# A three-round graph kernel: the rest rows of split chunks fetched by SyncE, where it fetched whole chunks

## The chip, the cores and the metric

The kernel runs on one core of a Trainium2 chip. The metric is the device time of one execution in microseconds (us); lower is better. Engines are called as in the profile: PE (TensorE), DVE (VectorE), ACT (ScalarE), POOL (GpSimd) and SP (SyncE).

## The reference

A graph has 12,500 nodes with 128 features and 200,000 edges, sorted by target node, each edge with a source node, one of four types and a weight. Cut to what matters:

```python
h = relu(layernorm(x))
ew = (w - w.min()) / (w.max() - w.min() + 1e-8)
# convolution 1 and 2 (relu between them): each edge takes its source's row,
# multiplied by the matrix of the edge's type, weighted, summed at the target
m = sum_r (type == r) * (h[src] @ W[r]);  out = segment_sum(m * ew, dst) + h @ root + b
x = x + conv2(relu(conv1(h)))
h = relu(layernorm(x))
x = x + segment_sum(w * h[src], dst) @ W3.T + b3
```

So there are three rounds over all edges, r = 0, 1, 2, and each must gather one row of 512 bytes for each edge.

## The kernel before

**Tiling.** The 200,000 edges are cut into 1,563 chunks of 128 edges (P = 128). Four chunks are a group (CG = 4), four groups a unit (UG = 4, UC = 16 chunks), and there are 98 units in a round (NU = 98). A ring of four units (RING = 4) of gathered rows stands in SBUF as `rows`, with 64 slots of 128 partitions by 128 floats.

**Gathering.** For each chunk POOL issues one indirect DMA (`gather`, L558), which reads 128 row numbers from a column of `idx` and brings 128 rows of 512 bytes from a table in HBM to one slot of `rows`. The tables are `table0` (round 0; its first four units gather from x), `table1` (round 1) and `table2` (round 2). DVE writes `idx` when a slot's unit of the last turn of the ring is done, and POOL waits for it (`s_idx`). At the second chunk of each group POOL also waits until PE has begun the group two before it (`paced`, `s_begun`, LEAD = 2).

**What POOL does not gather.** In units with u % 4 == 3 (`by_sp`; not u = 3 of round 0) the whole chunk 12 (SK) is fetched by SP: 128 DMAs of one row each, with addresses loaded from a list into registers eight at a time (`single_rows`, L502). They go to one of two buffers `spare`, and SP spreads them over the four units before (`singles`, a quarter of the 128 in each). In rounds 1 and 2, ACT fetches chunk 12 of units 17, 25, ... in the same way (`act_rows`, `spare_a`). That makes 71 chunks of SP, 22 of ACT, and 3 x 1,563 - 93 = 4,596 gathers of POOL.

**Use.** PE waits for each chunk's rows (`wait_rows`) and multiplies them with a window matrix that DVE built (L975 in round 0, L1016 in rounds 1 and 2). DVE adds the group's sums to `acc`. Tiles of nodes are then finished by PE, ACT and DVE, and SP stores them to the next table or to the output (`table1_out`, `table2_out`, `out_pair`). A round's gathers can begin only when the table before is complete.

**Order on SP.** SP's program has one order. In the setup: loads of x and of the edge lists, the weights, two lists for SP's own chunks and two for ACT's (`s_single_list`), then the 15 stores of `table0` (L418), each after ACT's `s_tab`. DVE waits for all four lists (`s_single_list` at 64) before it turns them to byte addresses (L1194 and following), and then starts on round 0. In the rounds, each unit's stores and loads are followed by the unit's share of single rows (`singles(r, u)`).

Of the kernel before, what the change touches and what calls it, by code (L numbers as in the profile page):

```python
# [4 lines left out]
P = 128  # L5
CG = 4
# [7 lines left out]
EARLY = 6  # L14
OB = 8
SE = 4
AE = 8
LEAD = 2
SETTLED = 12
# [4 lines left out]
def build(nc, x, src, dst, etype, weight, W1, root1, b1, W2, root2, b2, W3, b3, out):  # L24
# [44 lines left out]
    with ctx:  # L69
# [3 lines left out]
        def sem(name):  # L73
            return ctx.enter_context(nc.semaphore(name))
# [86 lines left out]
        s_single = [[sem(f"s_single{r}{b}") for b in range(2)] for r in range(3)]  # L161
        s_single_at = sem("s_single_at")
        s_single_list = sem("s_single_list")
        s_by_act = [sem(f"s_by_act{b}") for b in range(2)]
        s_idx_part, s_agg_part = sem("s_idx_part"), sem("s_agg_part")

# [66 lines left out]
        def by_sp(r, u):  # L233

            return u % SE == SE - 1 and (r > 0 or u >= SE)

        def is_single(r, u, k=SK):

            return k == SK and (by_sp(r, u) or by_act(r, u))

        def by_act(r, u):

# [19 lines left out]
        def wait_rows(eng, r, u, k):  # L262

            if u == NU - 1:
                eng.wait_ge(s_tail[k], 16 * (r + 1))
            elif is_single(r, u, k) and by_act(r, u):
                n = act_number(r, u)
                eng.wait_ge(s_by_act[n % 2], 16 * P * (n // 2 + 1))
            elif is_single(r, u, k):
                n = single_number(r, u // SE)  # L270
                so_far = len(range(n, single_number(r, 0 if r else 1) - 1, -2))
                eng.wait_ge(s_single[r][n % 2], 16 * P * so_far)
            elif k == SK:
                eng.wait_ge(rows_signal(u, k), single_gathers(r, u))
            elif k % CG < CG - 1:
                v = u % RING
                per_round = NI if v < last_units - 1 else NI - 1
                both = 2 if k % CG == CG - 2 else 1
                eng.wait_ge(s_row[v * UG + k // CG][k % CG], 16 * both * (r * per_round + u // RING + 1))

        def chunk_rows(r, u, k):

            if is_single(r, u, k) and by_act(r, u):
                return spare_a[:, act_number(r, u) % 2, :]
            if is_single(r, u, k):
                return single_buffer(single_number(r, u // SE))
            return rows[:, u % RING * UC + k, :]

        def paced(r, u, k):
# [63 lines left out]
        def _(eng):  # L353
# [127 lines left out]
            def single_rows(r, j, lo, hi):  # L481

                n = single_number(r, j)
                if lo == 0:
                    if n == 0:
                        eng.wait_ge(s_single_at, 7)
                    elif n > 1:
                        r0, j0 = divmod(n - 1, NO)
                        u = j0 * SE + SE - 1
                        if r0 == 0:  # L490
                            eng.wait_ge(s_half, 2 * u + 2)
                        else:
                            eng.wait_ge(s_agg, (r0 - 1) * NU + u + 1)
                numbers, table = single_at[r], in_bytes[r]
                to = single_buffer(n).bitcast(mybir.dt.uint8)
                for p in range(lo, hi, OB):
                    found = nc.values_load_multi_w_load_instructions(
                        numbers[j:j + 1, p:p + OB], engines=(mybir.EngineType.SP,), min_val=0,
                        max_val=table.shape[1] - row_bytes,
                        skip_runtime_bounds_check_because="the lists name nodes of the graph alone")[1]  # L500
                    for k in range(OB):
                        eng.dma_start(to[p + k:p + k + 1, :], table[0:1, bass.ds(found[k], row_bytes)]  # L502
                                      ).then_inc(s_single[r][n % 2], 16)

            def singles(r, u):

                if u < 2:
                    if r > 0:
                        single_rows(r, 0, u * P // 2, (u + 1) * P // 2)
                else:  # L510
# [36 lines left out]
        def _(eng):  # L547
# [9 lines left out]
            def gather(table, slot, signal):  # L557
# [291 lines left out]
        def _(eng):  # L849
# [99 lines left out]
            def first_round():  # L949
# [6 lines left out]
                def unit(i, v):  # L956
                    u = i * RING + v
                    for q in range(UG):
                        h = q // 2
                        if q in groups_of(u):  # L960
# [3 lines left out]
                            for k in range(n):  # L964
                                if not raw:
                                    wait_rows(eng, 0, u, q * CG + k)
                                if k == 0 and (raw or g == RING * UG):
# [31 lines left out]
            def fast(r):  # L999

                def unit(i, v):
# [5 lines left out]
                    for q in groups_of(u):  # L1007
# [3 lines left out]
                        for k in range(n):  # L1011
                            slot = v * UC + q * CG + k
                            wait_rows(eng, r, u, q * CG + k)
                            if k == CG - 1 and q == UG - 1 and RING - 1 <= u < NU - 1:
                                eng.wait_ge(s_window, u * 2 + ((r - 1) * 2 * NU + 4))
                            ins = eng.matmul(agg_of(u, v, q)[:, q * W:(q + 1) * W], chunk_rows(r, u, q * CG + k), window[:, slot, :],  # L1016
# [53 lines left out]
        def _(eng):  # L1070
# [446 lines left out]
```

## Time and profile before

| what | value |
|---|---|
| time, median of 2 runs | 7904.76 us (7901.24 to 7908.29) |
| profiled execution, first to last instruction (span) | 5774.9 us |
| POOL busy in the span | 4343.6 us, 75% |
| PE busy | 3158.5 us, 55% |
| DVE, ACT busy | 25%, 8% |
| gathers of POOL | 4,596 |
| one-row DMAs of SP, of ACT | 9,088 and 2,816 |

The span is 2,130 us shorter than the median of the runs. The profile shows nothing of what lies around the span, and no separate time of that one execution; the span is all that is known of it. Busy time of POOL counts its gathers while descriptors are made; "issue" is idle time in which an engine waited for nothing that the profile shows.

### The profile page before, as it was taken

What the parts mean: (1) busy time and instruction counts of PE and PEld (TensorE: products, weight loads), DVE (VectorE), ACT (ScalarE), POOL (GpSimd) and SP (SyncE); (2) the same over time, 40 slices, a digit from 0 to 9 for tenths busy, and PEclk for the clock granted to TensorE, in tenths of its full rate; (3) what the DMA queues carried; (4) which work ended last, traced back from release to release, by engine and by line L of the source; (5) the groups of instructions that cost most, each with busy time, mean ns of one, the idle gap of its engine ahead of it and who ended that gap; (6) DMA issues with size and microseconds to landing.
All of it is one profiled execution on the core that took longest, in us unless ns stands there. A gap on an engine that the chain in (4) does not pass through costs nothing.

```text
span 5774.9 us, 61089 instructions
## 1 busy us (share of the span) xinstructions
PE 3158.5 (55%) x11399; PEld 2521.8 (44%) x11399; DVE 1415.7 (25%) x5042; ACT 439.1 (8%) x1183; POOL 4343.6 (75%) x4604
## 2 busy tenths in 40 slices
PE   3766666666666545444444444444444445444454
PEld 2655544544555434333334443434444444444443
DVE  7433333333333222122212222211111111111111
ACT  5111111111111000000000000000000000000000
POOL 7777777777777677777777777777777777777777
PEclk7878788788877655555555555555555555555555
DMA  6222222222222222222222222222222222222222
GB/s 173 82 76 74 73 75 74 73 75 74 73 75 74 61 62 62 61 60 62 62 60 61 62 62 60 62 59 60 62 62 60 62 62 60 62 62 61 60 62 58
DMA packets 285830, 392.59 MB, mean 68 GB/s; under 512 B 92011, under 2 KB 199360, under 8 KB 285440
## 3 DMA queue, kind: packets, MB, share of 16 engines
q0 software_dynamic: 147072, 301.50, 20.0%
q1 hardware_dynamic: 132736, 85.70, 4.9%
q14 instruction: 299, 2.45, 0.1%
q8 instruction: 91, 1.49, 0.1%
q10 hardware_dynamic: 5632, 1.45, 0.1%
HBM read 336.95 MB, written 51.34 MB: 67 GB/s over the span
## 4 chain that ended last, share of the span: by engine, by line
POOL 74%; issue 24%; PE 1%; DMA 1%; DVE 0%; ACT 0%; POOLq 0%; DVEq 0%
POOL rows L558 74%; DMA rows<-table,idx 1%; PE bank L975 0%; PE bank L915 0%; PE bank L893 0%; PE bank L908 0%; PE bank L923 0%; DMA table<-st 0%; DMA table<-sums 0%; DMA st<-in_src_dram 0%; PE bank L924 0%; DVE win L1342 0%; PE bank L1016 0%; DVE acc L1223 0%; POOLq L69 0%
## 5 line engine op out<-in xcount | busy, mean ns | idle before, releaser
L558 POOL DMA_INDIRECT rows<-table,idx x4532 | 4276.9, 944 | 1402.1 <-issue 1378.0
L1016 PE MATMUL bank<-win,rows 128*128 128x48 f32 x6112 | 1816.9, 424 | 1938.7 <-DMA rows<-table,idx 1917.4
L1016 PEld LDWEIGHTS bank<-win,rows 128*128 128x128 f32 x6112 | 1474.6, 317 | 2281.5 <-DMA rows<-table,idx 2261.1
L975 PE MATMUL bank<-win,rows 128*128 128x192 f32 x3080 | 850.0, 404 | 634.9 <-DMA rows<-table,idx 490.2
L975 PEld LDWEIGHTS bank<-win,rows 128*128 128x128 f32 x3080 | 587.4, 226 | 846.9 <-DMA rows<-table,idx 670.2
L1223 DVE TENSOR_TENSOR acc<-acc,bank 128x48 f32 x1173 | 237.8, 203 | 1106.0 <-PE bank L893 956.6
L1342 DVE TENSOR_SCALAR win<-iota,key,sw_col 128x192 f32<-128x192 f32 x1563 | 501.5, 391 | 18.2 <-PE bank L908 16.2
L688 ACT ACTIVATE tile_T<-acc 128x128 f32<-128x128 f32 x196 | 60.4, 309 | 2852.5 <-DVE acc L1223 2852.5
L1285 DVE TENSOR_SCALAR idx<-src_col 128x16 int32<-128x16 int32 x98 | 18.5, 191 | 829.7 <-PE bank L1016 829.7
L893 PE MATMUL bank<-sums,W1s 128*128 128x192 f32 (+1 forms) x784 | 218.7, 445 | 0.4 <-ACT sums L736 0.4
L1372 DVE TENSOR_TENSOR bank<-bank,rel 128x384 f32<-128x384 f32 x392 | 218.6, 558 | 0.7 <-issue 0.2
L1292 DVE SCALAR_TENSOR_TENSOR idx<-src_col,type_col 128x16 int32<-128x16 int32 x98 | 18.5, 191 | 772.1 <-PE bank L1016 772.1
L893 PEld LDWEIGHTS bank<-sums,W1s 128*128 128x128 f32 x784 | 205.1, 280 | 0.9 <-ACT sums L736 0.9
L1273 DVE TENSOR_TENSOR st<-bank,x_rows 128x128 f32<-128x128 f32 x98 | 28.6, 292 | 709.3 <-PE bank L947 709.3
L1094 DVE BATCH_NORM_STATS2 stats<-bank 128x6 f32<-128x128 f32 x98 | 29.2, 299 | 677.9 <-PE bank L945 677.9
L915 PE MATMUL bank<-W2s,tile_T 128*128 128x512 f32 x194 | 147.9, 858 | 0.0
L1376 DVE TENSOR_TENSOR win<-bank,w_col 128x384 f32<-128x384 f32 x196 | 109.0, 556 | 6.8
L1376 DVE TENSOR_TENSOR win<-bank,sw_col 128x384 f32<-128x384 f32 x196 | 109.0, 556 | 6.8
L623 ACT ACTIVATE std<-mv,eps 128x1 f32<-128x1 f32 (+3 forms) x127 | 37.2, 293 | 822.3 <-DVE mv L1100 822.3
L701 ACT ACTIVATE acc<-bank,b2s 128x128 f32<-128x128 f32 x98 | 36.0, 367 | 740.8 <-PE bank L924 740.8
L736 ACT ACTIVATE sums<-bank 128x384 f32<-128x384 f32 x196 | 85.6, 495 | 5.6 <-PE bank L975 5.6
L678 ACT ACTIVATE hT<-bank 128x128 f32<-128x128 f32 x98 | 27.2, 277 | 756.6 <-PE bank L901 756.6
(123 smaller groups left out, 1235.4 us busy)
## 6 DMA issues: line engine op xcount, KB each, us to landing
spare<-table SPq DMA_DIRECT2D x9088, 0.5 KB
rows<-table,idx POOLq DMA_INDIRECT x4532, 2.5
spare_a<-table ACTq DMA_DIRECT2D x2816, 0.5 KB
table<-st SPq DMA_DIRECT2D x146, 256.0 KB, 2.4
x_rows<-table SPq DMA_DIRECT2D x49, 128.0 KB
x_rows<-in_x_dram SPq DMA_DIRECT2D x48, 128.0 KB
h_rows<-table SPq DMA_DIRECT2D x48, 128.0 KB, 2.3
out_dram<-st SPq DMA_DIRECT2D x48, 128.0 KB, 2.1
```

The lines of the kernel that those rows point to most:

```text
L558: eng.indirect_dma_start(out=rows[:, slot, :], out_offset=None, in_=table[:, :], in_offset=bass.IndirectOffsetOnAxis(ap=idx[:, slot:slot + ...
L623: eng.activation(std[:, p, 0:n], mv[:, p, 0:n, 1], ACT.Sqrt, bias=eps[:, 0:1]).then_inc(s_std, 1)
L688: eng.activation(tile_T[:, s, :], columns(t), ACT.Copy).then_inc(s_prep, 1)
L736: eng.activation(sums[:, v % 2, 2 * h:2 * h + w, :].rearrange("p g w -> p (g w)"), half_ps[v % 2 * 2 + h][:, 0:w * RW], ACT.Copy).then_inc ...
L893: ins = eng.matmul(mix_ps[:, 0:w], W1s[:, k, :], rhs(k), start=(k == 0), stop=(k == R - 1))
L915: eng.matmul(wide_of(t)[:, :], inner_of(t, s), W2s[:, :, :].rearrange("p r d -> p (r d)"), start=True, stop=True).then_inc(s_fin, 1)
L975: ins = eng.matmul(half_ps[v % 2 * 2 + h][:, q % 2 * RW:(q % 2 + 1) * RW], chunk_rows(0, u, q * CG + k), wide[:, v % 2, q * CG + k, :], st ...
L1016: ins = eng.matmul(agg_of(u, v, q)[:, q * W:(q + 1) * W], chunk_rows(r, u, q * CG + k), window[:, slot, :], start=(k == 0), stop=(k == n - 1))
L1223: eng.tensor_tensor(a, a, sums_ps, ALU.add).then_inc(s_acc, 1)
L1342: ins = eng.tensor_scalar(wide[:, v % 2, q * CG + k, :], iota[:, 0:RW], key0[:, bass.ds(c, 1)], sw_col[:, bass.ds(c, 1)], ALU.is_equal, AL ...
L1372: eng.tensor_tensor(match_ps[:, 0:n, :], iota_ps.unsqueeze(1).to_broadcast([P, n, W]), rel[:, bass.ds(c + lo, n)].unsqueeze(2).to_broadcas ...
L1376: eng.tensor_tensor(slots, match_ps[:, 0:n, :], wt[:, bass.ds(c + lo, n)].unsqueeze(2).to_broadcast([P, n, W]), ALU.mult).then_inc(s_windo ...
```

## The change

In each unit with u % 4 == 3 (again not u = 3 of round 0) POOL now issues a gather for all 16 chunks. In m of the 16 chunks the gather covers only the first n rows, and SP fetches the other 128 - n rows of these chunks, one DMA for each row, straight into their places in `rows`. The pair (m, n) goes through (1, 64), (2, 96), (4, 112), (8, 120), (16, 124), (16, 126), (16, 127) from one such unit to the next, so SP fetches 64, 64, 64, 64, 64, 32 and 16 rows of a unit, not 128. The chunks are 0, 16/m, 2 x 16/m and so on.

SP fetches a unit's rows in its program order at the two units u - 4 and u - 3, and only once PE is done with the unit that used the same slots (u - 4). PE waits for them at the unit's chunk 0 (`wait_parts`); before, it waited at chunk 12. In the setup the two lists are loaded by 2 + 48 small DMAs, with a wait of SP for the first two (`s_single_first`), and DVE waits for all of them. ACT's chunks stay as they are.

```diff
+PARTS = ((1, 64), (2, 96), (4, 112), (8, 120), (16, 124), (16, 126), (16, 127))
...
-            return k == SK and (by_sp(r, u) or by_act(r, u))
+            return k == SK and by_act(r, u)
+        def parts(u):
+            m, n = PARTS[u // SE % len(PARTS)]
+            return range(0, UC, UC // m), n
+        def rows_by_pool(r, u, k):
+            if not by_sp(r, u):
+                return P
+            of, n = parts(u)
+            return n if k in of else P
...
+        def wait_parts(eng, r, u, k):
+            if by_sp(r, u) and k == parts(u)[0][0]:
+                n = single_number(r, u // SE)
+                mine = range(n, single_number(r, 0 if r else 1) - 1, -2)
+                eng.wait_ge(s_single[r][n % 2], 16 * sum(rows_by_sp(r, ((i + 1) - r * NO) * SE + SE - 1) for i in mine))
...
-                              ).then_inc(s_single_list, 16)
+                              ).then_inc(s_single_first, 16)
+            eng.wait_ge(s_single_first, 32)
+            for to, arr in ((single_src, src), (single_type, etype)):
+                for j in range(NO):
+                    u = j * SE + SE - 1
+                    of, n = parts(u)
+                    eng.dma_start(to[j:j + 1, 0:len(of) * (P - n)].rearrange("a (m e) -> a m e", m=len(of)),
+                                  arr[u * UC * P:(u + 1) * UC * P].rearrange("(m c e) -> m c e", m=len(of), e=P)[:, 0, n:P].unsqueeze(0),
+                                  allow_slow_non_contiguous=n == P - 1).then_inc(s_single_list, 16)
...
-                for p in range(lo, hi, OB):
+                for p in range(lo, min(hi, len(of) * each), OB):
...
-                        eng.dma_start(to[p + k:p + k + 1, :], table[0:1, bass.ds(found[k], row_bytes)]
-                                      ).then_inc(s_single[r][n % 2], 16)
+                        slot, row = u % RING * UC + of[(p + k) // each], by_pool + (p + k) % each
+                        to = rows[row:row + 1, slot, :].bitcast(mybir.dt.uint8)
+                        eng.dma_start(to, table[0:1, bass.ds(found[k], row_bytes)]).then_inc(s_single[r][n % 2], 16)
...
-                if u < 2:
-                    if r > 0:
-                        single_rows(r, 0, u * P // 2, (u + 1) * P // 2)
-                else:
-                    j, part = divmod(u + 2, SE)
-                    if 0 < j < NO:
-                        single_rows(r, j, part * P // SE, (part + 1) * P // SE)
+                j, part = divmod(u + 1, SE)
+                if j < NO and by_sp(r, j * SE + SE - 1) and part < 2:
+                    single_rows(r, j, 0 if u == 0 else part * P // 4, (part + 1) * P // 4)
...
-                    out=rows[:, slot, :], out_offset=None, in_=table[:, :],
-                    in_offset=bass.IndirectOffsetOnAxis(ap=idx[:, slot:slot + 1], axis=0)).then_inc(signal, 16)
+                    out=rows[0:n, slot, :], out_offset=None, in_=table[:, :],
+                    in_offset=bass.IndirectOffsetOnAxis(ap=idx[0:n, slot:slot + 1], axis=0)).then_inc(signal, 16)
...
-                        gather(table, v * UC + k, rows_signal(u, k))
+                        gather(table, v * UC + k, rows_signal(u, k), rows_by_pool(r, u, k))
...
-            eng.wait_ge(s_single_list, 64)
+            eng.wait_ge(s_single_list, 32 + 32 * NO)
```

## Rows read from the trace of the kernel before

**Rows 1.** The page: the chain that ended last, by engine, then by line.

```profile
POOL 74%; issue 24%; PE 1%; DMA 1%; DVE 0%; ACT 0%; POOLq 0%; DVEq 0%
```

**Rows 2.** The source line L558: durations ns min/median/max, releasers (us, times), landing.

```profile
L558 POOL DMA_INDIRECT rows<-table,idx x4532: 940/944/1071, 88.1 to 5765.9; - x198
...
  issue: 1397.2, 4581
  DMA table<-sums: 12.0, 1
  DMA table<-st: 8.5, 1
  PE bank L975: 3.7, 12
...
DMA to landing us min/median/max: 2.4/2.5/7.0
```

**Rows 3.** Timeline of POOL in round 2: start us, us, instruction, idle before it.

```profile
5000.57 0.95 POOL L558 DMA_INDIRECT rows<-table,idx  x1 [0.30 <-issue]
...
5041.79 0.95 POOL L558 DMA_INDIRECT rows<-table,idx  x1 [0.30 <-issue]
```

**Rows 4.** Windows of 500 us, one in each round: busy us (count) by engine, clock, DMA.

```profile
1000.00:1500.00 500.00, 333.77 (x1245) 250.12 (x1245) 158.31 (x550) 58.92 (x154) 377.73 (x402) 0.82 0.27 74
2500.00:3000.00 500.00, 247.24 (x845) 199.29 (x846) 102.88 (x381) 27.28 (x77) 377.65 (x402) 0.50 0.23 61
4500.00:5000.00 500.00, 247.58 (x872) 205.84 (x872) 82.89 (x259) 8.04 (x26) 378.02 (x401) 0.50 0.23 61
```

**Rows 5.** Waits, all engines: who waited for whom, us, times, longest.

```profile
PE bank L1016 <- DMA rows<-table,idx: 1917.4, 1773, 7.9
```

**Rows 6.** The page: DMA queues, packets, MB, share of 16 engines' span.

```profile
q0 software_dynamic: 147072, 301.50, 20.0%
```

**Rows 7.** Timeline of SP's queue at the start of round 1 and in it.

```profile
1944.15 45.84 SPq L502 DMA_DIRECT2D spare<-table  x105
```

**Rows 8.** Waits of SP's queue, whole span: us, times, longest.

```profile
SPq L471 <- DVE st L1273: 514.8, 46, 39.0
SPq L444 <- DVE st L1238: 473.7, 46, 38.5
SPq L428 <- ACT st L712: 424.2, 85, 19.7
```

**Rows 9.** Timeline of SP's queue in the setup.

```profile
12.93 0.23 SPq L372 DMA_DIRECT2D win<-in_src_dram  x1
...
44.31 0.40 SPq L409 DMA_DIRECT2D single_src<-in_src_dram  x1
...
46.02 30.67 SPq L418 DMA_DIRECT2D table<-acc  x15
79.79 16.92 SPq L388 DMA_DIRECT2D h_rows<-table  x3
```

**Rows 10.** Waits of SP's queue from 0 to 320 us.

```profile
SPq L418 <- ACT acc L628: 20.2, 8, 2.9
```

**Rows 11.** The page: a first load's size and time to landing.

```profile
st<-in_src_dram SPq DMA_DIRECT2D x1, 64.0 KB, 1.8
```

**Rows 12.** Timeline of DVE in the setup and the first unit.

```profile
71.09 0.42 DVE L1194 TENSOR_SCALAR single_at<-single_src 24x128 int32<-24x128 int32 x1
...
84.35 0.23 DVE L1301 COPY idx<-src_col 128x8 int32<-128x8 int32 x1
```

**Rows 13.** Timeline of POOL at its first gather from table0.

```profile
86.87 0.94 POOL L558 DMA_INDIRECT rows<-in_x_dram,idx  x1 [0.30 <-issue]
88.12 0.94 POOL L558 DMA_INDIRECT rows<-table,idx  x1 [0.30 <-issue]
```

More of the change, by code:

```diff
@@ L163, in build @@
         s_single_list = sem("s_single_list")
+        s_single_first = sem("s_single_first")
         s_by_act = [sem(f"s_by_act{b}") for b in range(2)]
@@ L237, in is_single, with rows_by_sp @@
         def is_single(r, u, k=SK):
-            return k == SK and (by_sp(r, u) or by_act(r, u))
+            return k == SK and by_act(r, u)
[7 more added lines that the diff above has]
+            return n if k in of else P
+        def rows_by_sp(r, u):
+            of, n = parts(u)
+            return len(of) * (P - n)
         def by_act(r, u):
@@ L268, in wait_rows @@
                 eng.wait_ge(s_by_act[n % 2], 16 * P * (n // 2 + 1))
[L269 to L272, printed above, removed]
             elif k == SK:
@@ L284, in chunk_rows @@
                 return spare_a[:, act_number(r, u) % 2, :]
-            if is_single(r, u, k):
-                return single_buffer(single_number(r, u // SE))
             return rows[:, u % RING * UC + k, :]
@@ L409, in _ @@
                 eng.dma_start(to[:, :], arr[0:last].rearrange("(j c e) -> j c e", c=SE * UC, e=P)[:, (SE - 1) * UC + SK, :]
-                              ).then_inc(s_single_list, 16)
+                              ).then_inc(s_single_first, 16)
[3 more added lines that the diff above has]
+                    u = j * SE + SE - 1
+                    of, n = parts(u)
+                    eng.dma_start(to[j:j + 1, 0:len(of) * (P - n)].rearrange("a (m e) -> a m e", m=len(of)),
+                                  arr[u * UC * P:(u + 1) * UC * P].rearrange("(m c e) -> m c e", m=len(of), e=P)[:, 0, n:P].unsqueeze(0),
+                                  allow_slow_non_contiguous=n == P - 1).then_inc(s_single_list, 16)
             for to, arr in ((act_src, src), (act_type, etype)):
@@ L483, in single_rows @@
                 n = single_number(r, j)
+                u = j * SE + SE - 1
+                of, by_pool = parts(u)
+                each = P - by_pool
                 if lo == 0:
@@ L486, in single_rows @@
                         eng.wait_ge(s_single_at, 7)
[L487 to L491, printed above, removed]
-                        else:
-                            eng.wait_ge(s_agg, (r0 - 1) * NU + u + 1)
+                    r0, before = (r, u - RING) if u >= RING else (r - 1, u + (NU - 1) // RING * RING - RING)
+                    if r0 == 0:
+                        eng.wait_ge(s_half, 2 * before + 2)
+                    else:
+                        eng.wait_ge(s_agg, (r0 - 1) * NU + before + 1)
                 numbers, table = single_at[r], in_bytes[r]
-                to = single_buffer(n).bitcast(mybir.dt.uint8)
-                for p in range(lo, hi, OB):
+                for p in range(lo, min(hi, len(of) * each), OB):
                     found = nc.values_load_multi_w_load_instructions(
@@ L501, in single_rows @@
                     for k in range(OB):
-                        eng.dma_start(to[p + k:p + k + 1, :], table[0:1, bass.ds(found[k], row_bytes)]
-                                      ).then_inc(s_single[r][n % 2], 16)
+                        slot, row = u % RING * UC + of[(p + k) // each], by_pool + (p + k) % each
+                        to = rows[row:row + 1, slot, :].bitcast(mybir.dt.uint8)
+                        eng.dma_start(to, table[0:1, bass.ds(found[k], row_bytes)]).then_inc(s_single[r][n % 2], 16)
             def singles(r, u):
-                if u < 2:
-                    if r > 0:
-                        single_rows(r, 0, u * P // 2, (u + 1) * P // 2)
-                else:
-                    j, part = divmod(u + 2, SE)
-                    if 0 < j < NO:
-                        single_rows(r, j, part * P // SE, (part + 1) * P // SE)
+                j, part = divmod(u + 1, SE)
+                if j < NO and by_sp(r, j * SE + SE - 1) and part < 2:
+                    single_rows(r, j, 0 if u == 0 else part * P // 4, (part + 1) * P // 4)
             for u in range(NU):
@@ L555, in _, with gather @@
                      allow_small_or_imprecise_dtypes=True).then_inc(s_const, 1)
-            def gather(table, slot, signal):
+            def gather(table, slot, signal, n=P):
                 eng.indirect_dma_start(
-                    out=rows[:, slot, :], out_offset=None, in_=table[:, :],
-                    in_offset=bass.IndirectOffsetOnAxis(ap=idx[:, slot:slot + 1], axis=0)).then_inc(signal, 16)
+                    out=rows[0:n, slot, :], out_offset=None, in_=table[:, :],
+                    in_offset=bass.IndirectOffsetOnAxis(ap=idx[0:n, slot:slot + 1], axis=0)).then_inc(signal, 16)
             def gather_unit(table, r, i, v):
@@ L966, in unit @@
                                     wait_rows(eng, 0, u, q * CG + k)
+                                    wait_parts(eng, 0, u, q * CG + k)
                                 if k == 0 and (raw or g == RING * UG):
@@ L1013, in unit @@
                             wait_rows(eng, r, u, q * CG + k)
+                            wait_parts(eng, r, u, q * CG + k)
                             if k == CG - 1 and q == UG - 1 and RING - 1 <= u < NU - 1:
```

## The prediction

> **What bounds the kernel now.** I read the chain of work that ended last first: 74% of it is POOL and 24% is issue, the stretches before POOL's own gathers; nothing else reaches 2% [rows 1]. Then the gather's source line: each of the 4,532 gathers from a table takes 940 to 1,071 ns, median 944, and nearly all the idle time ahead of them is issue, 1,397 us in 4,581 pieces, so 0.305 us each [rows 2]. The timeline gives the sum directly: from 5000.57 to 5041.79 us there are 33 gathers, 41.22 / 33 = 1.249 us from one start to the next [rows 3]. The windows say that this holds in all rounds, whatever PE does: 401 or 402 gathers in every 500 us, with PE at 334 us busy in round 0 and at 247 in the others, and at a granted clock of 0.82 or 0.50 [rows 4]. 4,596 x 1.249 = 5,740 us of a span of 5,775. The rest is the start and the two table changes, where POOL waited 12.0 and 8.5 us [rows 2]. The waits show the other side: PE stood 1,917 us for gathered rows in rounds 1 and 2 alone [rows 5]. So POOL sets the span by the number of gathers and by what one costs.
>
> The timed runs are 7,905 us, 2,130 more than the span, and no view says what that is. I take it as a part that the change leaves alone, and carry the other reading as a rival. The sum below is made on the span and then added to 7,905. This kernel's measurement can tell about 2% (158 us) from no change.
>
> **The change: POOL.** Before, POOL left out one chunk in each of 71 units (24 in a round, 23 in round 0). Now it leaves out none: 71 more gathers, 4,667 in all. At 1.249 us each that is +88.7 us, all on the path, since POOL waits for nothing else.
>
> Against that stand shorter gathers. In seven such units 1 + 2 + 4 + 8 + 16 + 16 + 16 = 63 gathers are cut, by 368 rows in all. A round has three such turns and the first three units of a fourth: 196 cut gathers and 1,296 rows; over the kernel, less the one unit of round 0, 587 gathers and 3,824 rows. Every gather of the trace has 128 rows, so the price of a row is bounded only: if the length doesn't depend on rows, 0; if all of the 1.249 us does, 9.76 ns a row, 37.3 us in all; and if the 944 ns busy alone do, 7.4 ns and 28.2 us. The narrow band of 940 to 1,071 ns [rows 2] says that the cost is software of fixed length, but not in which loop. I take half of the busy part, 14 us, and keep 0 and 37. A gather of an odd number of rows might instead cost more than one of 128; no row excludes it and no row prices it, so it goes to the rivals.
>
> The first thing to see here is that leaving out one whole chunk takes 1.249 us off POOL for 128 rows of SP, while the same SP rows spread over many gathers take at most that and perhaps nothing. The Trainium skill ("DMA: Bandwidth & Descriptors", section "Anatomy of one DMA — SWDGE (gpsimd) path") calls descriptor generation small and variable and says that one can emit a lot of descriptors before the incremental cost shows up. By that rule the saving is 0 and the POOL term 88.7 in place of 74.6; the trace has one size of gather only and neither agrees nor disagrees.
>
> **SP and the new wait.** SP's one-row DMAs fall from 9,088 to 3,824. One costs SP 45.84 / 105 = 0.437 us with its address loads [rows 7]. That frees 5,264 x 0.437 = 2,300 us of SP, none of it on the path: SP already waited over 1,400 us for tiles to store [rows 8]. Gain 0.
>
> Of a unit u, SP now starts only when PE has finished u - 4, since the rows go into ring slots. It then needs at most 64 x 0.437 = 28 us plus a landing of about 2.5 us. PE wants them at chunk 0 of unit u, three units or 47 gathers later, 47 x 1.249 = 59 us (48 if ACT fetches none). Cover: 28 us to spare; without it PE would wait and POOL would follow after its lead. Behind the waiting SP stand the stores of finished tiles and the reloads of `x_rows`; those of rounds 1 and 2 come up to one unit (20 us) later. They have two staging slots of a pair of tiles each, 40 us of work a turn, and SP's waits of up to 39 us for tiles [rows 8] show it far ahead. Price 0; at worst, some us at the end of a round, but the last unit with SP rows is 95 and its rows are issued at 91 and 92. So the table changes stay at 12.0 and 8.5 us.
>
> PE's own work is the same matmuls, and its waits are filled by POOL's pace; 0.
>
> **The setup.** SP gets a wait and 48 list DMAs ahead of the stores of table0. The nearest issue times are 0.23 us for a one-row load and 0.40 for the 24-row list [rows 9]: 11 to 19 us. The wait costs about a landing, 1.8 us [rows 11], plus little. The stores started at 46.0 and would start at 59 to 68. They took 30.7 us [rows 9], of which 20.2 were waits for ACT [rows 10], so 10.5 us of issue alone: at worst they end at 78.5, where they ended at 76.7. POOL wants table0 at 88.1 [rows 13], and SP had it at 79.8 [rows 9]; cover 8 us, of which 2 are used. DVE wants the lists at 71.1 [rows 12]; they land at 61 to 70. Here the cover is thin, 1 us at the upper end. If each DMA cost double the 0.40, DVE would be late by 19 us; the index copy for unit 4 came at 84.35 [rows 12] for a gather at 88.12, 3.8 us of cover, so POOL would lose some 15. I take +2, with 0 and 15 as bounds.
>
> **Sum.** 88.7 - 14 + 2 = +77 us: span 5,852, time 7,982 us. Bounds: 88.7 - 37.3 = +51, and 88.7 + 15 = +104; times 7,956 to 8,009.
>
> **Rivals.**
> 1. The unseen 2,130 us scale with the gathers, as if one cost 7,905 / 4,596 = 1.72 us outside the profile. For it: the gathers fill the span, so whatever stretches the execution must stretch them or stand apart. Against: nothing shows it. Then 77 x 1.37 = +105: 8,010, and 7,975 to 8,047 with the bounds.
> 2. Gathers of uneven size go to fewer DMA engines (slower than before). A gather of 128 rows uses 20.0% x 16 x 5,775 / 4,596 = 4.0 us of engine time [rows 6], spread so well that it lands after 2.5 us [rows 2]. If 127 rows all go to one engine and always the same one, a unit with 16 such gathers takes 16 x 4.0 = 64 us, where POOL needs 20. POOL may lead PE by some nine gathers (11 us), so about 33 us are lost in each of the nine units 27, 55 and 83 of three rounds: +300, time 8,280. It decides from the point where engine time per gather, over the engines that take turns, passes 1.249 us: four or more in turn cost nothing but a later landing. The other form is a longer gather instruction: the 504 gathers of 120 to 127 rows would have to cost 0.16 us more each to reach 2%. The Trainium skill ("DMA: Bandwidth & Descriptors", section "Why a DMA increments its semaphore by 16 and not by 1") says that the number of engines is the largest up to 16 that divides the partitions, one for 127, taken in turn by a round-robin cursor for POOL's DMAs. By that rule, with the turn, the time stays with the forecast and the landing in those units goes to about 6 us; the trace shows 128 rows only.
> 3. POOL is not what binds the timed runs. If the 2,130 us are another engine's, PE's say, the added gathers are hidden: 7,905. If they were SP's row DMAs, of which 58% vanish, the time would fall by more than 2%. Against both: SP stood idle over 1,400 us in the profiled execution [rows 8] and PE over 1,900.
> 4. The cut gathers become much shorter: to be over 2% faster, 587 of them would have to save (158 + 77) / 587 = 0.40 us each beyond the 14 us, when most lose 1 to 8 rows. Nearly excluded; a part of it, a saving of 0.15 us each, would end at about 7,894.
>
> **Chances.** Forecast 60%; rival 1, 18%; rival 2, 13% (of the rest of its range, 8,070 to 8,350); rival 3, 6%, half of it faster by over 2%; rival 4, 3%. Only rival 2 and a very dear setup end over 2% slower (above 8,063): 0.14. Faster by over 2% (below 7,747): 0.04. Within 2%: 0.82. For the range I take the forecast and rival 1 with their bounds and the unchanged time of rival 3, with some room for a light form of rival 2: 7,895 to 8,080.
>
> **What would show it.** In the profile after: 4,667 gathers; the median of a full gather still 944 ns with 0.30 us ahead; those of 64 rows between 0.47 and 0.95 us, those of 127 at about 0.94; POOL busy up by 39 to 67 us; SP's row DMAs at 3,824; no wait of PE for them at chunk 0; the first table gather at 88 us. I am wrong if gathers of 120 to 127 rows take another length, if landings in units 27, 55 and 83 make POOL wait for PE, if DVE stands for the lists near 71 us, or if the time and the span move by different amounts.

## The result: 7,174 us, where 7,982 was forecast

The changed kernel takes 7174.5 us (median of two runs, 7173.5 to 7175.5) against 7904.8 before: 0.907 of it, 95% interval 0.903 to 0.910. The forecast was +1%, with a range from 7,895 to 8,080.

The first surprise stands in the head of the profile after. Its span is 7,173.7 us, as long as its time; nothing lies around it. So it is likely that the 2,130 us between span and time of before were no part outside the span either, and that the one profiled execution of before, 5,775 us, was of another kind than its timed runs; set 3 below shows both. The chain, in the page of the changed kernel, answers to [rows 1]:

```profile
issue 35%; POOL 23%; SPq 21%; another core or an unknown queue 14%; DVE 3%; PE 2%; DMA 1%; ACT 1%; ACTq 0%; DVEq 0%
```

SP's queue, which was not on the chain of before, has 21% of it. Of the 35% issue, 26 lie directly before SP's own instructions, so 47% belong to SP; POOL with the issue before it has 29%. The source line of the gather in the changed kernel, L583, answers to [rows 2]:

```profile
L583 POOL DMA_INDIRECT rows<-table,idx x4603: 899/944/2566, 157.6 to 7162.1; - x192
L583 POOL DMA_INDIRECT rows<-in_x_dram,idx x64: 940/944/1594, 4.1 to 83.6; - x64
...
  issue: 1343.6, 4379
  remote: 625.7, 193
  PE bank L1043: 312.5, 79
  DVE idx L1328: 102.0, 4
```

Three things are to be seen. There are 4,667 gathers, as worked out. The median is still 944 ns and the issue ahead of it about 0.31 us, so a whole gather costs the same as in [rows 2, 3]. But the longest takes 2,566 ns, and POOL now waits over 1,000 us for others ("remote" is a signal whose sender the trace does not name), where it waited for 25 us before. PE in turn waits 515 us for SP's rows, in the waits of the same profile:

```profile
PE bank L1043 <- DMA rows<-table: 514.7, 34, 17.4
```

The windows, against [rows 4], show it as 331 to 341 gathers in 500 us, not 401:

```profile
1000.00:1500.00 500.00, 284.67 (x1015) 218.99 (x1014) 135.14 (x445) 47.46 (x124) 343.85 (x331) 0.73 0.23 61
2500.00:3000.00 500.00, 198.91 (x703) 163.84 (x703) 86.57 (x324) 22.59 (x64) 327.02 (x341) 0.50 0.19 51
```

SP's queue in round 1 and in the setup, against [rows 7] and [rows 9]:

```profile
53.47 37.32 SPq L436 DMA_DIRECT2D single_src<-in_src_dram  x24
91.74 17.34 SPq L436 DMA_DIRECT2D single_type<-in_edge_type_dram  x24
...
3137.68 39.92 SPq L532 DMA_DIRECT2D rows<-table  x32
```

A row costs SP 39.92 / 32 = 1.25 us here, where [rows 7] gave 0.437. Over this whole trace the row DMAs start 1.15 us apart on average (pauses of over 6 us left out), over the first profile of before 0.44. That is the lead that the experiments follow.

### The profile page after: what moved, and what is told of

Its sections match the earlier page's. It is cut to its first block, busy times and chain, and to the rows that moved or that the text cites. A ratio compares the mean times of both kernels' runs of the same rounds, so it can differ in the third digit from the quotient of the medians.

```text
span 7173.7 us, 50093 instructions
## 1 busy us (share of the span) xinstructions
PE 3185.0 (44%) x11399; PEld 2579.1 (36%) x11399; DVE 1431.5 (20%) x5042; ACT 439.9 (6%) x1183; POOL 4695.6 (65%) x4675
## 4 chain that ended last, share of the span: by engine, by line
issue 35%; POOL 23%; SPq 21%; another core or an unknown queue 14%; DVE 3%; PE 2%; DMA 1%; ACT 1%; ACTq 0%; DVEq 0%
POOL rows L583 23%; SPq L532 18%; SPq L525 2%; DVE win L1369 1%; DMA rows<-table,idx 1%; PE bank L1001 1%; PE bank L1043 1%; PE bank L918 0%; DVE acc L1250 0%; DMA rows<-table 0%; ACT acc L653 0%; ACTq L823 0%; SPq L479 0%; DVE stats L1121 0%
## 5 line engine op out<-in xcount | busy, mean ns | idle before, releaser
L583 POOL DMA_INDIRECT rows<-table,idx x4603 | 4632.2, 1006 | 2446.3 <-issue 1324.4
L1043 PE MATMUL bank<-win,rows 128*128 128x48 f32 x6208 | 1776.1, 421 | 2697.8 <-DMA rows<-table,idx 1992.5
L1043 PEld LDWEIGHTS bank<-win,rows 128*128 128x128 f32 x6208 | 1479.8, 320 | 3000.8 <-DMA rows<-table,idx 2282.9
L1001 PE MATMUL bank<-win,rows 128*128 128x192 f32 x3126 | 908.6, 428 | 937.5 <-DMA rows<-table,idx 433.8
L1001 PEld LDWEIGHTS bank<-win,rows 128*128 128x128 f32 x3126 | 653.2, 244 | 1147.6 <-DMA rows<-table,idx 577.0
L1369 DVE TENSOR_SCALAR win<-iota,key,sw_col 128x192 f32<-128x192 f32 x1563 | 526.0, 407 | 88.8 <-remote 77.8
L918 PE MATMUL bank<-sums,W1s 128*128 128x192 f32 (+1 forms) x784 | 245.2, 485 | 68.2 <-ACT sums L761 61.4
L918 PEld LDWEIGHTS bank<-sums,W1s 128*128 128x128 f32 x784 | 220.4, 301 | 80.3 <-ACT sums L761 72.9
L1313 DVE COPY idx<-src_col 128x16 int32<-128x16 int32 x90 | 17.8, 198 | 651.7 <-remote 539.7
L1133 DVE RECIPROCAL rstd<-std 128x1 f32<-128x1 f32 (+3 forms) x127 | 23.6, 186 | 363.5 <-ACT std L648 205.7
```

Source lines behind the costliest of these rows:

```text
L583: eng.indirect_dma_start(out=rows[0:n, slot, :], out_offset=None, in_=table[:, :], in_offset=bass.IndirectOffsetOnAxis(ap=idx[0:n, slot:sl ...
L918: ins = eng.matmul(mix_ps[:, 0:w], W1s[:, k, :], rhs(k), start=(k == 0), stop=(k == R - 1))
L1001: ins = eng.matmul(half_ps[v % 2 * 2 + h][:, q % 2 * RW:(q % 2 + 1) * RW], chunk_rows(0, u, q * CG + k), wide[:, v % 2, q * CG + k, :], st ...
L1369: ins = eng.tensor_scalar(wide[:, v % 2, q * CG + k, :], iota[:, 0:RW], key0[:, bass.ds(c, 1)], sw_col[:, bass.ds(c, 1)], ALU.is_equal, AL ...
```

## The experiments

They ran in five sets, each on one chip with runs of the kernel before beside it. In sets 1 and 5 that kernel took 5,777 us, as long as its first profile; in sets 2, 3 and 4 it took 7,816, 7,915 and 7,900 us, close to the pair on record. I call the chips of sets 1 and 5 **quick** and the others **slow**; the sets ran on four chips (sets 2 and 3 on the same one). No chip was seen in both kinds, so the words name what was measured there at that time; that it is a lasting property of a chip is not shown. All times are medians.

| kernel | rows by SP | quick | slow |
|---|---|---|---|
| before | 9,088 | 5,777 | 7,816 / 7,915 / 7,900 |
| changed | 3,824 | 6,172 | 7,160 / 7,176 / 7,177 |
| no rows by SP | 0 | 5,864 | 6,846 |
| no rows by SP or ACT | 0 | 5,891 | 6,849 |
| (1, 64) throughout | 4,544 | 5,867 | 7,014 |
| SE = 8 | 4,480 | not run | 6,827 |
| before, OB = 2 | 9,088 | not run | 9,505 |
| changed, OB = 2 | 3,824 | not run | 7,669 |
| changed, other sizes (set 2) | 2,152 | not run | 6,882 (one run) |

### Set 1 (quick): the kernel before again, and POOL alone

> The kernel before, unchanged, for a second profile. Theory S (SP binds): in the timed runs a row DMA of SP costs 7,905 / 9,088 = 0.87 us and not the 0.437 of the first profile, so its queue is never at rest; the new profile has a span of about 7,900 us, as long as the time, POOL idle for some 2,100 us more than in the first, and L502 at 0.85 us or more a row. Theory O (the rest lies outside the span): the span is again near 5,775 us, with 2,130 us around it. Theory G (gathers are longer in timed runs): span 7,900 us, gathers at 1.7 us each without idle time between them.

5776.7 us, ratio 1.000 (0.999 to 1.001); span 5,774.5. On this chip time and span agree, and the first profile of before is a true picture. None of the three theories was right as put: the same kernel, profiled or timed, takes 5,777 us here and took 7,905 in the pair on record.

```diff
         def by_sp(r, u):
-            return u % SE == SE - 1 and (r > 0 or u >= SE)
+            return False
...
         def singles(r, u):
+            return
```

> The kernel before, with SP's 71 chunks gathered by POOL and no row DMA on SP: 4,667 gathers. Theory S: POOL binds, 4,667 x 1.249 + 35 = 5,864 us; up to 200 more if ACT's row DMAs are as slow as SP's and hold up the tiles. Theory O: 7,905 + 89 = 7,994 us. Theory G: 7,905 x 4,667 / 4,596 = 8,027 us.

5864.2 us, 1.015 (1.014 to 1.017): the sum 4,667 x 1.249 + 35 to the microsecond.

```diff
         def by_act(r, u):
-            return r > 0 and u % AE == 1 and AE < u < AO * AE
+            return False
...
         def act_rows(r, u):
+            return
```

> As the kernel with no row DMA on SP, and ACT's 22 chunks gathered by POOL as well: 4,689 gathers, no row DMA at all. Theory S: 4,689 x 1.249 + 35 = 5,892 us, below the one with ACT's rows if ACT's rows are slow too, 28 us above it if they are free. Theory O: 7,905 + 117 = 8,022 us. Theory G: 8,065 us.

5891.1 us, 1.020 (1.018 to 1.022); again the sum. So on a quick chip POOL binds and a whole gather is worth 1.249 us, as the prediction had it.

```diff
-PARTS = ((1, 64), (2, 96), (4, 112), (8, 120), (16, 124), (16, 126), (16, 127))
+PARTS = ((1, 64),)
```

> The changed kernel with (1, 64) in every fourth unit: no gather of 120 to 127 rows, but 4,544 row DMAs on SP in place of 3,824, all 64 of a unit between the end of unit u - 4 and the start of unit u. If the uneven gathers are what is left to lose, 144 x (2.542 - 0.944) + 144 x (1.282 - 0.944) = 279 us less and the time falls to about 6,900 us. If SP's rows and the wait for them bind in every unit, the period of four units stays at the 92 us that the changed kernel has for (1, 64), 73.5 x 92 = 6,760 us. If rows cost nothing, 5,870 us.

5866.7 us, 1.016 (1.014 to 1.017): the case "rows cost nothing". 71 added gathers give 88.7 us, their 64 missing rows take off 71 x 0.041 = 2.9, and the start adds about 3; +90.2 was measured. The new wait at chunk 0 costs nothing on a quick chip, as predicted. SP's queue in the setup of this kernel, where each list is one run of numbers:

```profile
47.88 7.06 SPq L436 DMA_DIRECT2D single_src<-in_src_dram  x24
54.98 7.56 SPq L436 DMA_DIRECT2D single_type<-in_edge_type_dram  x24
63.33 22.33 SPq L446 DMA_DIRECT2D table<-acc  x15
```

48 DMAs in 14.6 us, 0.30 each, and the stores of table0 begin at 63.3, inside the predicted 59 to 68.

### Set 2 (slow): the changed kernel, other sizes, dearer rows

> The changed kernel, unchanged, beside the kernel before on one chip. Theory S (the pair on record was measured where SP's and ACT's row DMAs cost about twice as much; where a row costs 0.44 us POOL binds both kernels): 5,776.5 + 71 x 1.249 + what its profile gave for cut gathers (11 x -42, 24 x -29, 48 x -16, 72 x +35, 144 x +338, 144 x +38, 144 x +1,598 ns = +284.8 us) = 6,150 us, 6.5% slower than before. Rival (the change itself takes 9% off, and the first profile of before misled): 7,174 us or 0.907 of before on this chip, 5,238 us.

7159.5 us, 0.917 (0.914 to 0.920) of before's 7,816: this chip is a slow one, and the gain of the pair on record came back. It said nothing yet of a quick one.

```diff
-PARTS = ((1, 64), (2, 96), (4, 112), (8, 120), (16, 124), (16, 126), (16, 127))
+PARTS = ((8, 127), (4, 122), (8, 123), (2, 124), (8, 125), (2, 116), (2, 100), (8, 121))
```

> The changed kernel with other (m, n): (8, 127), (4, 122), (8, 123), (2, 124), (8, 125), (2, 116), (2, 100), (8, 121). If a gather's length goes with the number of DMA engines, k the largest divisor of n up to 16, as 838 + 1,704 / k ns (through 944 for 128 and 2,542 for 127, which gives 1,264 for 124 where 1,282 was measured): 127 at 2,542, 122 (k = 2) at 1,690, 123 (3) at 1,406, 124 and 116 (4) at 1,264, 125 (5) at 1,179, 100 (10) at 1,008, 121 (11) at 993 ns. If instead odd counts are dear and even ones cheap: 121, 123, 125 near 2,542 and 122 near 980.

POOL's timeline in round 1, one gather of each of 127, 122, 123, 124, 125, 116, 100 and 121 rows:

```profile
2443.96 2.56 POOL L583 DMA_INDIRECT rows<-table,idx  x1 [0.30 <-issue]
...
2544.16 1.67 POOL L583 DMA_INDIRECT rows<-table,idx  x1 [0.30 <-issue]
...
2632.80 1.42 POOL L583 DMA_INDIRECT rows<-table,idx  x1 [0.30 <-issue]
...
2726.72 1.30 POOL L583 DMA_INDIRECT rows<-table,idx  x1 [0.30 <-issue]
...
2815.29 1.20 POOL L583 DMA_INDIRECT rows<-table,idx  x1 [0.30 <-issue]
...
2907.51 1.27 POOL L583 DMA_INDIRECT rows<-table,idx  x1 [0.30 <-issue]
...
2997.48 1.00 POOL L583 DMA_INDIRECT rows<-table,idx  x1 [0.30 <-issue]
...
3091.33 1.01 POOL L583 DMA_INDIRECT rows<-table,idx  x1 [0.30 <-issue]
```

The formula 838 + 1,704 / k ns gives 2.54, 1.69, 1.41, 1.26, 1.18, 1.26, 1.01 and 0.99 us; every one is met within 0.04. It was put through 128 and 127 rows; the other sizes test it. It is k, the largest divisor of n up to 16, and not odd or even: 121 is odd and cheap, 122 even and dear. A second form fits all 14 sizes of these runs as well or better: 0.86 us + 13.3 ns x n / k, within 0.03. It also gives the 0.902 us of 64 rows, where the first says 0.944. The runs do not separate the two further.

The single run of this kernel took 6,882 us, with 2,152 rows on SP and 64 gathers of 127 rows where the changed kernel has 3,824 and 144: 278 us below that one in the same set.

```diff
-OB = 8
+OB = 2
```

> The kernel before with OB = 2: addresses are loaded two at a time and not eight, so a row of SP costs (0.82 + 0.07 + 2 x 0.32) / 2 = 0.77 us, ACT's rows alike. Theory S: SP binds, 9,088 x 0.77 = 7,000 us and up to 7,300 with its stores. If SP is off the path whatever a row costs: 5,777 us.

> The changed kernel with OB = 2. Theory S: 64 rows x 0.77 = 49 us fit into the 59 us between the end of unit u - 4 and the start of unit u, so POOL still binds: 6,150 us as with OB = 8, up to 6,300 where stores come late, and so 12 to 16% faster than the kernel before with the same OB, while with OB = 8 it is slower. If the wait for rows at chunk 0 is what counts: over 6,700 us.

9504.7 us, 1.217 (1.213 to 1.221) of before with OB = 8, and 7668.5 us. Both numbers were missed, since 0.77 us is the price of a quick chip. What they show is what more loads of addresses cost the time on a slow one: 4,544 loads in place of 1,136 add (9,505 - 7,816) / 3,408 = 0.50 us each to the kernel before, and 1,912 in place of 478 add (7,669 - 7,160) / 1,434 = 0.35 us each to the changed one. ACT's loads grew fourfold in both too, from 352 to 1,408, so the price is not SP's alone; but SP's queue, with the issue before its instructions, is 96% of the chain of the kernel before with OB = 2, and 68% of that of the changed one. So SP's queue binds the kernel before there outright, and the changed one for a part. With dear rows the change takes 19% off (7,669 / 9,505).

### Set 3 (slow): a profile of before, and its parts

> The kernel before once more, for its profile on the chip of this set. On a chip where rows cost 0.43 us: 5,777 us, POOL busy 75%. On a chip where the kernel before takes over 7,700 us: theory S wants a span as long as the time, SP's queue without rest (waits far under the 1,400 us of the first profile), 7,816 / 9,088 = 0.86 us a row on average, gathers still at 944 + 305 ns, and POOL idle for some 2,000 us more, ended by PE, which in turn stands for the rows in spare.

7919.6 us, 1.001 of before; span 7,907.9. The chain in the page of this second profile of before, with its first entries by line:

```profile
SPq 58%; issue 37%; another core or an unknown queue 2%; DVE 1%; ACT 1%; PE 0%; DMA 0%; POOL 0%; DVEq 0%; ACTq 0%
SPq L502 47%; SPq L497 10%; SPq L388 0%; SPq L428 0%; DVE stats L1094 0%; ACT acc L628 0%; SPq L445 0%; PE bank L975 0%; SPq L451 0%; POOL rows L558 0%; DVE win L1342 0%; SPq L471 0%; ACT rows L628 0%; DMA rows<-table,idx 0%
```

POOL has 0% of it. SP's row DMAs (L502) with their address loads (L497) have 57%, and all but 1% of the 37% issue lies directly before SP's own instructions, so SP's queue makes 95% of the chain. SP's queue in the timeline of the same profile:

```profile
3020.87 74.93 SPq L502 DMA_DIRECT2D spare<-table  x64
3096.29 0.05 SPq L445 DMA_DIRECT2D table<-st  x1
3097.74 35.41 SPq L502 DMA_DIRECT2D spare<-table  x64
```

64 rows take 75 and 35 us in these two bursts (28 by [rows 7]), and with a store between them the next burst begins when the last one ends. Over the trace the row DMAs start 0.83 us apart on average and so fill 7,559 of the 7,908 us. The gather's source line there has the same length of a gather and a new wait:

```profile
L558 POOL DMA_INDIRECT rows<-table,idx x4532: 938/944/1095, 152.0 to 7896.9; - x198
...
  issue: 1304.7, 4212
  PE bank L1016: 1304.0, 151
```

And PE, in the waits of that profile, stands for SP's rows:

```profile
PE bank L1016 <- DMA spare<-table: 1227.4, 48, 33.8
```

SP's largest wait for tiles, 515 us in 46 pieces in [rows 8], is 32 us in two here, and all its waits together fall from 1,532 to 213 us. So the ring is: SP late with its rows, PE late, POOL stopped by its pace.

> The changed kernel beside it. Where rows cost 0.43 us: 5,776.5 + 88.7 + 284.8 = 6,150 us, slower by 6.5%. Where the kernel before takes over 7,700 us: 7,160 us again, faster by 8 to 9%.

7176.0 us, 0.907 (0.905 to 0.908).

> No row DMA on SP, 4,667 whole gathers, ACT's rows as before. Where rows cost 0.43 us: 5,864 us again. Where the kernel before takes over 7,700 us: theory S wants POOL back as the bound, 5,864 us, and up to 300 more if ACT's 16 rows a unit at 1.0 us (16 of the unit's 20 us) make its tiles late. A theory in which something else of that chip is slow (HBM, gathers, PE) wants over 7,000 us.

6846.4 us, 0.865 (0.864 to 0.866): 1,068 us off, which is what SP's rows cost there. But the other 982 us down to 5,864 stayed: theory S in its first form fell, and the rival theory, which wanted over 7,000 us, was missed too. Units of round 0, in which nobody issues row DMAs, took 23 us. PE's and POOL's timeline of that kernel in one of them, and ACT's:

```profile
1514.23 0.27 PE L902 MATMUL bank<-ident,h_rows 128*128 128x128 f32 x1
...
1524.94 0.28 ACT L679 ACTIVATE hT<-bank 128x128 f32<-128x128 f32 x1 [13.11 <-remote]
...
1525.21 0.94 POOL L559 DMA_INDIRECT rows<-table,idx  x1 [3.19 <-remote]
```

ACT copies (L679) what PE transposed (L902); the transpose ended at 1514.50 and the copy began at 1524.94, 10.4 us later, and POOL stood from 1522.02 to 1525.21, 0.27 us past that moment. It is no single case: the copy begins over 1 us after the transpose in 81 of the 98 tiles, median 10.2 us and longest 15.7 us. On a quick chip, in the first profile of before, the pair is 0.04 us apart in all 98:

```profile
1007.33 0.27 PE L901 MATMUL bank<-ident,h_rows 128*128 128x128 f32 x1
...
1007.64 0.28 ACT L678 ACTIVATE hT<-bank 128x128 f32<-128x128 f32 x1 [6.01 <-PE bank L901]
```

> The changed kernel with (1, 64) throughout: no uneven gathers, 4,544 rows on SP. Where rows cost 0.43 us: 5,867 us. Where the kernel before takes over 7,700 us: 64 rows at 1.0 to 1.2 us are 64 to 77 us, more than the 59 us between the end of unit u - 4 and the start of unit u, so PE waits in each such unit: 92 to 94 us a turn of four units (what the changed kernel had there for (1, 64)), 73.5 x 93 = 6,840 us. If the uneven gathers alone made the rest: 7,160 - 285 = 6,875 us, too close to tell; the periods of four units in the profile have to.

7014.1 us, 0.886 (0.884 to 0.887), 174 us above the sum that I gave and 162 below the changed kernel. It has 720 more rows than that one and no uneven gathers. My expectation left the decision to the periods of four units, and the traces have them. The median time from POOL's first gather of a unit to that of the fourth unit after it, in rounds 1 and 2 (quick: sets 1 and 5, slow: this set), by what the SP unit among the four has:

| SP unit | quick, us | slow, us |
|---|---|---|
| no rows by SP | 79.3 | 90.7 |
| (1, 64) throughout | 79.3 | 94.4 |
| changed kernel: (1, 64) | 79.9 | 94.4 |
| changed: (4, 112) | 78.7 | 95.2 |
| changed: (16, 124) | 84.1 | 98.7 |
| changed: (16, 126) | 80.5 | 91.1 |
| changed: (16, 127) | 104.3 | 111.6 |

A unit of 127-row gathers costs about 20 us more than one of 126 on a slow chip, in nine units some 185 us, and 24 us on a quick one. So uneven gathers cost a little less on a slow chip, part of them falling into time in which POOL waits anyway. A unit with 64 rows of SP costs 3.7 us there, and nothing on a quick chip. The likely reason stands in the waits of (1, 64) throughout: PE waits 46 times for SP's rows, and these rounds have 48 such units.

```profile
PE bank L1043 <- DMA rows<-table: 705.5, 46, 18.7
```


### Set 4 (slow): is ACT the rest, and does the place of the wait count

> No row DMA at all, 4,689 whole gathers. On a chip where rows cost 0.43 us: 5,891 us again. On the other chip, theory S in its first form (row DMAs alone are slow there) wants 5,892 us, 950 below the kernel that still has ACT's rows; theory T (everything but POOL's gathers is slower there, signals of PE come up to 10 us late, and units of round 0, which have no row DMAs, took 23 us and not 20) wants nearly the same 6,850 us, within 100.

6849.0 us, 0.867 (0.865 to 0.868), as theory T wanted. Its "everything but POOL's gathers" is too wide: DVE and ACT are busy for 1,413 and 439 us in this profile, as in the first one of before. ACT's rows are not the rest; without any row DMA a slow chip is still 958 us behind a quick one.

```diff
-SE = 4
+SE = 8
```

> The kernel before with SE = 8: SP fetches a whole chunk in every eighth unit, 35 chunks or 4,480 row DMAs, nearly as many as (1, 64) has, spread over eight units and awaited at chunk 12; POOL issues 36 gathers more than before. Where rows cost 0.43 us: 5,776.5 + 36 x 1.249 = 5,821 us, 45 below (1, 64) for as many rows. On the other chip: if the number of rows counts, 7,014 us as with (1, 64); if the wait at chunk 0 behind the end of unit u - 4 counts as well, less, down to 6,846 - 36 x 1.25 = 6,800 us.

6827.3 us, 0.864 (0.863 to 0.866), the lowest time on a slow chip. About as many rows as with (1, 64), and 187 us less. 35 gathers fewer (SP has 35 whole chunks) account for 44 us of that; so some 140 us come from how (1, 64) does it: 64 rows in a burst that may begin only at the end of unit u - 4 and are awaited at chunk 0. The profiles agree: with SE = 8 PE never waits for SP's rows, though they start 1.29 us apart, and SP's queue has no part in the chain; with (1, 64) PE waits the 706 us above. The two ran on different slow chips, on which the changed kernel took the same time, and the burst and the wait were not tried apart.

> The changed kernel again. Where rows cost 0.43 us (not yet measured there): 5,776.5 + 88.7 + 284.8 = 6,150 us, 6.5% slower than before. On the other chip 7,160 to 7,176 us, 0.907 to 0.917 of before.

7176.6 us, 0.908 (0.907 to 0.910).

### Set 5 (quick): the changed kernel at last

> The changed kernel again, for a chip where a row costs SP 0.43 us and the kernel before takes 5,777 us: 6,150 us, 6.5% slower (88.7 us for 71 gathers, 284.8 for the cut ones). A wait at chunk 0 that bites there would add to it. On a chip where the kernel before takes over 7,700 us: 7,176 us.

6172.3 us against 5,776.7, 1.068 (1.067 to 1.070): **slower**. The gather's source line in this profile of the changed kernel:

```profile
L583 POOL DMA_INDIRECT rows<-table,idx x4603: 900/944/2606, 104.5 to 6161.7; - x192
...
  issue: 1416.9, 4647
  DMA table<-acc: 18.0, 1
  DMA table<-sums: 12.0, 1
  DMA table<-st: 8.6, 1
  PE bank L1001: 4.6, 15
  DVE idx L1328: 2.2, 1
...
DMA to landing us min/median/max: 2.3/2.6/9.1
```

POOL waits for PE 4.6 us in all, so the later landings cost nothing (a gather of 127 rows lands 7.9 us after its start in the median, up to 9.1, where about 6 was worked out). What is new is one wait of 18.0 us for table0. POOL's timeline has each kind of unit; here the first gathers of 64, 124, 126 and 127 rows in round 1:

```profile
2146.99 0.90 POOL L583 DMA_INDIRECT rows<-table,idx  x1 [0.30 <-issue]
...
2464.53 1.29 POOL L583 DMA_INDIRECT rows<-table,idx  x1 [0.30 <-issue]
...
2549.89 0.98 POOL L583 DMA_INDIRECT rows<-table,idx  x1 [0.30 <-issue]
...
2629.17 2.55 POOL L583 DMA_INDIRECT rows<-table,idx  x1 [0.31 <-issue]
```

And the setup, SP's queue and then DVE:

```profile
48.69 14.60 SPq L436 DMA_DIRECT2D single_src<-in_src_dram  x24
63.32 14.84 SPq L436 DMA_DIRECT2D single_type<-in_edge_type_dram  x24
...
79.11 21.59 SPq L446 DMA_DIRECT2D table<-acc  x15
```

```profile
80.83 0.22 DVE L1221 TENSOR_SCALAR single_at<-single_src 24x128 int32<-24x128 int32 x1 [9.62 <-DMA act_type<-in_edge_type_dram]
```

The account on a quick chip, with the median of each size over all its gathers: 71 more gathers 88.7 us; 144 of 127 rows at 2.542 us +230.1; 144 of 124 at 1.282 us +48.7; 144 of 126 at 0.982 us +5.5; 72 of 120 at 0.979 us +2.5; those of 64, 96 and 112 at 0.902, 0.915 and 0.928 us -2.0; POOL's wait for table0 and its index 18.0 + 2.2. Sum +393.7; measured 6172.3 - 5776.7 = +395.6.

## Why the prediction was wrong, step by step

**What bounds the kernel.** The step that failed is the one after the chain: "I take it as a part that the change leaves alone", of the 2,130 us. With it the term "Gain 0" for SP's 5,264 row DMAs failed. On the chips of the timed runs SP binds the kernel before: with its rows gone the time falls by 1,068 us, half of the gap, and its own profile there gives SP's queue, with the issue before its instructions, 95% of the chain and POOL none. In place of +88.7 from the gathers and 0 from SP, the change measured 730 us less. Rival 3 had this in one sentence ("if they were SP's row DMAs ... the time would fall by more than 2%") and got 3%, on the ground that SP stood idle for 1,400 us. But that idleness was read from the profile whose span already contradicted the times; on a slow chip all of SP's waits are 213 us. Rival 1 falls: whole gathers take 944 ns in the slow profiles too. So does rival 4: a gather of 64 rows saves 0.04 us.

**The gain.** On a slow chip: 5,264 fewer rows bring the kernel from SP's pace to where SP is a part of the bound only: 7,915 to 7,176. Of the 1,068 us that SP's rows cost, the change regains 740. Of the other 330, some 185 are gathers of 127 rows, by the periods of four units. The remaining 145 or so hold the rows that PE awaits and the gathers of 124 rows; the runs do not part them further, and the sum is loose, since these overlap with waits.

**The added gathers.** 71 x 1.249 = 88.7 us was right where POOL binds: +87.7 was measured with no rows on SP.

**The price of a row.** I took 14 us off, half of the busy time. The runs give (944 - 902) / 64 = 0.66 ns a row where k is 16, which would be 2.5 us for all 3,824 rows. With that the rule quoted from the Trainium skill ("DMA: Bandwidth & Descriptors", section "Anatomy of one DMA — SWDGE (gpsimd) path"), that descriptor generation is small, agrees. With 127 rows the same instruction takes 2.54 us, and for that "small" does not hold.

**Uneven gathers.** "No row excludes it and no row prices it" was true, another length of the gathers of 120 to 127 rows stood among my signs of being wrong, and yet the range took nothing for it: I gave this second form of rival 2 the same 13% as the first. It costs 284.8 us on a quick chip, 230 of them in the 144 gathers of 127 rows. Its first form fell: units of 127-row gathers took no more than POOL's own time for them, and POOL waited for PE 4.6 us in all. The Trainium skill ("DMA: Bandwidth & Descriptors", section "Why a DMA increments its semaphore by 16 and not by 1") has the number of engines as the largest divisor up to 16; I used it for the landing and missed that it could set the length of the instruction. The times of six sizes that the change does not have agree with that divisor, at 1.7 / k us above a floor of 0.84. That the engines are the reason is not shown; the runs show the divisor.

**The setup.** Predicted +2 with 0 to 15, measured +20.2. Each list DMA took 29.4 / 48 = 0.61 us on average, not 0.23 to 0.40, though 0.30 where each list is one run: most lists of the change are 2 to 16 runs (0.57 to 0.67 us each, whatever the number), and I had priced them by loads of one run a partition; so the stores of table0 began at 79.1 and not at 59 to 68, and DVE stood 9.6 us for the lists. I had even priced the double issue time, but only for DVE, and not for the stores behind it, whose cover of 8 us it uses up first. A second term was too small: I took 10.5 us for the 15 stores without their waits for ACT. They took 21.6 us with no such wait in the profile, 1.44 us each; that makes some 11 of POOL's 18 us.

**SP and the new wait** cost nothing on a quick chip, as predicted: (1, 64) throughout lands on the POOL sum. On a slow one the cover of 28 us was not there: rows start 1.15 to 1.22 us apart, so 64 of them take over 70 us where 59 are free, and PE waits 515 us for them in the changed kernel.

**What stays open.** Why a slow chip is slow. Without any row DMA the kernel is still 958 us behind there. SP's queue goes in steps of 0.7 us and its double there, with row DMAs in the kernel or without. Here are two of the weights' loads in the setup of the changed kernel, 1.40 us apart; on a quick chip most of them are 0.3 to 0.6 us apart:

```profile
44.37 0.69 SPq L425 DMA_DIRECT2D W3s<-in_L_gnn_W_dram  x1
45.77 0.69 SPq L425 DMA_DIRECT2D b3z<-in_L_gnn_b_dram  x1
```

And what waits for PE begins up to 16 us late. One more difference stands in the traces: for the same kernel before, a quick profile holds 110,762 records of semaphore updates and the slow one 32,318. So on a slow chip the names of who released whom rest on a part of the signals ("remote" is common there), and the surer evidence for SP is the 7,559 us that its rows fill. Whether one cause loses records and holds the queues up, or the recording itself holds them up, no run here tells.

## What to carry to other kernels

When the profiled span and the timed median differ by more than a few per cent, the profile may be of another kind of execution: every idle time and cover read from it is open. Here the engine that looked idle, with 9,088 one-row DMAs, was half of the difference. A gather by POOL should have a number of rows with a large divisor up to 16: in these runs k of 10 or more kept it under 1.02 us, while 127 rows made the instruction 2.7 times as long as 128. Leaving rows out saved next to nothing (0.04 us for half of them), so only whole gathers were worth taking away. A change that trades one queue's work for another's needs a time on each kind of chip: this one is 8 to 9% faster or 7% slower.

## What the runs showed of the hardware

- The length of an indirect gather of 512-byte rows follows the largest divisor k of its rows up to 16: 2.54 us (127 rows, k = 1), 1.67 (122, 2), 1.41 (123, 3), 1.28 (124, 4), 1.20 (125, 5), 1.00 (100, 10), 1.01 (121, 11), 0.98 (126 and 120, 14 and 15), 0.94 (128, 16) and 0.90 (64, 16).
- The same program takes 5,777 us on two chips and 7,816 to 7,915 on two others, steadily within each set. Whole gathers are the same 944 to 947 ns on all. SP's one-row DMAs start 0.44 us apart in the quick profiles; in the slow ones the distance is not one number: 0.83 us in the kernel before, 1.15 in the changed one, 1.29 with SE = 8.
- A list load into a single partition cost SP 0.30 us with one run of numbers (0.47 between loads of more runs), and 0.57 to 0.67 with 2 to 16 runs, without growing with their number.
- 15 stores of table0 (up to 448 KB) took SP 21.6 us back to back, 1.44 us each. In the first profile of before, where most of them came after a wait for ACT, eight took 0.37 us each.
